# Decoder layer on one core: v goes to k's bank, y is turned a group ahead, the causal term is narrowed, the last norm's rows go to ScalarE, and the end is reordered

## The reference

```python
x = norm(x + attn(x))      # linear attention of 16 heads, then an MLP 128 -> 512 -> 128 with a gelu on a grid of 0.1
x = norm(x + xattn(x, ctx, mask))
x = norm(x + ffn(x))

# xattn: 16 heads of 8 features, 64 keys of the same batch
q, k, v = x @ WQ, ctx @ WK, ctx @ WV
scores = q @ k.T / sqrt(8)
scores = where(mask[query] or key > query, -1e9, scores)
out = (softmax(scores) @ v) @ WO

# ffn: 7 gate scores; the two largest of their softmax are divided by their sum
out = x @ W_shared.T + (w0 + w1) * (x @ W_expert.T) + bias
```

## Time and profile before

| | |
|---|---|
| median of 3 runs | 562.51 us |
| profiled execution | 561.41 us |
| its span, first to last instruction | 559.7 us |
| mean granted TensorE clock | 0.973 |
| TensorE, VectorE, ScalarE, GpSimd busy | 88%, 72%, 65%, 67% |

### The profile page before, as it was taken

How to read it: one execution, slowest core, us unless ns; L and a number is a source line. 1 busy time by engine, 2 the same in 40 slices (tenths; PEclk the granted TensorE clock), 3 DMA queues, 4 the chain that set the end, 5 groups by cost and what they waited for, 6 DMA issues and landing times. The chain is left out here.

```text
span 559.7 us, 22010 instructions
## 1 busy us (share of the span) xinstructions
PE 491.0 (88%) x8800; PEld 365.4 (65%) x8800; DVE 404.7 (72%) x1406; ACT 363.9 (65%) x685; POOL 374.7 (67%) x686
## 2 busy tenths in 40 slices
PE   2899999998999999997899999899998999998750
PEld 1777777775777767774567667676676666766530
DVE  2677777755777776556678878688887888888764
ACT  1566666555777777747777677677677676777432
POOL 6566666645577774833337878778787887879553
PEclk9999999999999999999999999899999999999775
DMA  6530000000000000002000111111201121010001
GB/s 167 169 117 2 3 2 1 4 2 1 2 0 3 1 1 1 2 7 49 17 23 4 50 51 26 28 50 50 49 6 49 51 50 50 5 51 21 22 2 57
DMA packets 24742, 17.38 MB, mean 31 GB/s; under 512 B 2112, under 2 KB 22464, under 8 KB 24640
## 3 DMA queue, kind: packets, MB, share of 16 engines
q1 hardware_dynamic: 24208, 15.90, 10.7%
q10 hardware_dynamic: 432, 0.07, 0.1%
HBM read 11.77 MB, written 4.19 MB: 29 GB/s over the span
## 5 line engine op out<-in xcount | busy, mean ns | idle before, releaser
L783 ACT ACTIVATE gel<-gel,row_scale 128x512 f32<-128x512 f32 x96 | 66.1, 720 | 29.2 <-DVE gel L1056 19.0
L790 ACT ACTIVATE gel<-pair 128x1024 f32<-128x1024 f32 x64 | 51.8, 809 | 29.0 <-PE pair L1414 28.5
L1354 PEld LDWEIGHTS pair<-w,gel 128*128 128x128 f32 x512 | 60.4, 192 | 8.0 <-issue 5.7
L1043 DVE TENSOR_REDUCE neg_max<-pair 128x16 f32<-128x1024 f32 x64 | 60.5, 945 | 5.1 <-PE pair L1368 5.0
L1354 PE MATMUL pair<-w,gel 128*128 128x128 f32 x512 | 62.4, 276 | 1.0 <-ACT gel L715 1.0
L1318 PE MATMUL pair<-hT,w 128*128 128x512 f32 x128 | 58.3, 596 | 1.3 <-ACT lev L710 1.3
L1414 PE MATMUL pair<-ident,gel 128*128 128x128 f32 x384 | 55.7, 280 | 2.9 <-ACT gel L783 1.9
L532 POOL TENSOR_SCALAR k_exp<-k_sb,quad_mask 128x512 f32<-128x512 f32 x64 | 43.0, 690 | 20.8 <-ACT k_sb L762 12.7
L1414 PEld LDWEIGHTS pair<-ident,gel 128*128 128x128 f32 x384 | 43.4, 141 | 19.1 <-issue 13.5
L1368 PE MATMUL pair<-k_exp,qT 32*32 32x128 f32 (+1 forms) x2048 | 44.5, 333 | 2.6 <-issue 2.4
L509 POOL TENSOR_TENSOR X<-X,proj_sb 128x512 f32<-128x512 f32 x16 | 20.3, 1270 | 35.6 <-ACT proj_sb L673 35.6
(11 more groups left out here) (138 smaller groups left out, 1221.9 us busy)
## 6 DMA issues: line engine op xcount, KB each, us to landing
X<-in_x SPq DMA_DIRECT2D x16, 256.0 KB, 3.1
cT<-in_ctx SPq DMA_DIRECT2D x16, 256.0 KB, 3.9
out_rows<-X SPq DMA_DIRECT2D x15, 256.0 KB, 2.4
mask_rows<-in_mask_early SPq DMA_DIRECT2D x16, 128.0 KB, 3.6
w<-in_L_attn_w SPq DMA_DIRECT2D x2, 256.0 KB, 3.4
out_rows<-X SPq DMA_DIRECT2D x2, 128.0 KB, 1.8
w_kv<-in_L_attn_wk SPq DMA_DIRECT2D x1, 64.0 KB, 3.3
w_q<-in_L_attn_wq ACTq DMA_DIRECT2D x1, 64.0 KB, 3.1
```

What stands on the lines that cost most here:

```text
L783: nc.scalar.activation(part, part, ACT.Exp, scale=row_scale[:, n:n + 1])\
L790: nc.scalar.activation(pT[par].rearrange("p (a c) -> p a c", a=2), turned, ACT.Copy)\
L1043: nc.vector.tensor_reduce(neg_max[par][:, :].rearrange("p (a h) -> p a h", a=2), scores, AX.X, ALU.max, negate=True).then_inc(max_ready, 1)
L1354: last = nc.tensor.matmul(bank(6 + q)[:, P * t:P * (t + 1)], gel[:, q, f, P * t:P * (t + 1)], w_2[:, f, :], start=(f == 0), stop=(f == NF ...
```

## The change

- v's projection writes bank 5 (k's) in 16 products of 64 columns by 64 (before: 4 of 128 by 128 to bank 4), so that both halves of the heads lie on the partitions where `v2` wants them, and `copy_v` takes 2 instructions of 64x512 in place of 4 of 64x256.
- y is turned in slot 3 for group s+2 (before: in slot 0 for group s+1), and `copy_y` on ScalarE moves with it.
- The causal term of the even tile covers the last 32 keys of each head alone. It comes last in `scores_close`; that of the odd tile comes between the two halves of `scores_open`.
- The last norm's rows (`last_rows`) are made on ScalarE for every group, in slot 1 of step s for group s-3. GpSimd makes the scale and the offset (`last_offset`). The store of a group is a step later.
- In `end`, the mixture of group 14 is done by VectorE, and `add_bias(LAST)` comes ahead of the offsets of group 14.
- `MOE_BANK` is [6, 4, 5, 5], and the waits that go with the banks are moved. In slot 0, `turn_attended` comes ahead of the `moe` product, and on ScalarE `attT` ahead of `collect`.

```diff
-MOE_BANK = [5, 6, 4, 5]
+MOE_BANK = [6, 4, 5, 5]
...
@@ phase3 and end of GpSimd
                 if exists(s - 2) and s < LAST:
                     mixture(s - 2, p)
-                    last_norm(s - 2, p)
+                    last_offset(s - 2)
...
-                mixture(LAST - 1, q)
-                end_offset(LAST - 2, rstd_c, offs_b[0])
-                end_offset(LAST - 1, rstd_b[1], offs_b[1])
+                add_bias(LAST - 1, q)
+                last_offset(LAST - 2)
                 add_bias(LAST, 2)
+                last_offset(LAST - 1)
                 pool.wait_ge(ln_c.done, LAST - 1)
-                ln_deviation(pool, ln_c, LAST, mv_c, veps_c, rstd_c)
+                ln_deviation(pool, ln_c, LAST, mv_c, veps_c, rstd_c[LAST % 2])
...
+            def last_offset(g):
+                rstd, offs = rstd_c[g % 2], offs_b[g % 2]
+                after(pool, ln_c.done, g - 1)
                 ln_deviation(pool, ln_c, g, mv_c, veps_c, rstd)
@@ copy_v and phase3 of ScalarE
-                for b in range(2):
-                    for h in range(2):
-                        batches = v2[q][h * S:(h + 1) * S, :, :, h, 0:DH] \
-                            .rearrange("p (u b) i e -> p u b i e", b=2)
-                        last = nc.scalar.activation(batches[:, :, b, :, :],
-                                                    values[b * S:(b + 1) * S, :, h, :, :], ACT.Copy)
+                for h in range(2):
+                    rows = slice(h * S, (h + 1) * S)
+                    last = nc.scalar.activation(
+                        v2[q][rows, :, :, h, 0:DH],
+                        bank(first_bank(g, 5))[rows, :].rearrange("p (b i e) -> p b i e", i=HH, e=DH),
+                        ACT.Copy)
...
-                    if t == 0 and exists(nxt):
-                        copy_y(nxt)
+                    if t == 0 and exists(s - 2):
+                        collect((s - 2) * TG + TG - 1, TG - 1, p)
...
+                    if t == TG - 1 and exists(s + 2):
+                        copy_y(s + 2)
...
+                    if t == 1 and exists(s - 3):
+                        last_rows(s - 3)
@@ end of VectorE
                 gate_weights(LAST - 1)
+                mixture(LAST - 1, q)
                 gate_top(LAST, 2)
+                last_statistics(LAST - 1, q)
                 gate_weights(LAST)
-                last_statistics(LAST - 1, q)
@@ scores on TensorE
                 for n in ns:
-                    future_scores(n)
-                for n in ns:
+                    if n % 2:
+                        future_scores(n)
                     quad_scores(n, (1, 3) if n % 2 else (0, 2)).then_inc(s_opened, 1)
...
                 for n in ns:
-                    quad_scores(n, (0, 2) if n % 2 else (1, 3)).then_inc(s_done, 1)
+                    last = quad_scores(n, (0, 2) if n % 2 else (1, 3))
+                    if n % 2:
+                        last.then_inc(s_done, 1)
+                if ns[0] % 2 == 0:
+                    future_scores(ns[0]).then_inc(s_done, 1)
...
-                for u in range(TG):
-                    last = nc.tensor.matmul(bank(first_bank(g, 4))[:, P * u:P * (u + 1)],
-                                            cT[q][:, P * u:P * (u + 1)], w_xv[:, :], start=True, stop=True)
+                for u in range(2 * TG):
+                    for h in range(2):
+                        last = nc.tensor.matmul(bank(first_bank(g, 5))[h * S:(h + 1) * S,
+                                                                       FH * u:FH * (u + 1)],
+                                                cT[q][:, S * u:S * (u + 1)],
+                                                w_xv[:, FH * h:FH * (h + 1)],
+                                                start=True, stop=True)
@@ phase3 of TensorE
-                    if t == 0 and exists(g):
-                        after(pe, moe_ready, (s - 1) * TG - 1)
-                        after(pe, v2_ready, g)
-                        turn_y(g)
...
                     if t == 2 and exists(g):
+                        pe.wait_ge(k_ready, g + 1)
+                        project_v(g, q)
+                    if t == 3 and exists(s + 2):
                         pe.wait_ge(q_ready, g + 1)
-                        project_v(g, q)
+                        turn_y(s + 2)
...
                         for u in range(TG - 1):
+                            if u == 1 and exists(g):
+                                pe.wait_ge(yT_ready, min(s + 3, NG))
```

More of the change, by code:

```diff
@@ L115, in decoder_layer @@
         veps_c = sb("veps_c", [P, TG])
-        rstd_c = sb("rstd_c", [P, TG])
+        rstd_c = [sb(f"rstd_c{i}", [P, TG]) for i in range(2)]
         negm_c = sb("negm_c", [P, TG])
@@ L411, in phase3 @@
                     load_ctx(s + 2, p)
-                if exists(s - 2) and s - 2 < LAST:
-                    store(s - 2)
-            pipeline(sp, phase3, last=NG)
+                if exists(s - 3) and s - 3 < LAST:
+                    store(s - 3)
+            pipeline(sp, phase3, last=NG + 1)
             for k, part in halves:
@@ L816, in phase3 @@
                         copy_pT(s * TG + t, t % 2)
-                    if t == 0 and exists(s - 2):
-                        collect((s - 2) * TG + TG - 1, TG - 1, p)
+                    if s == 0 and t == 0:
+                        copy_y(1)
                     if t == 0 and exists(prev):
@@ L843, in phase3, with last_rows @@
                             collect(prev * TG + u, u, q)
-            def end_rows(g, q, rstd, offs):
-                act.wait_ge(end_offs, g - LAST + 3)
+            def last_rows(g):
+                q, rstd, offs = g % 2, rstd_c[g % 2], offs_b[g % 2]
+                act.wait_ge(offs_ready, g + 1)
                 for t in range(TG):
@@ L872, in end @@
                 gate_exp(LAST)
-                end_rows(LAST - 2, p, rstd_c, offs_b[0])
-                end_rows(LAST - 1, q, rstd_b[1], offs_b[1])
+                last_rows(LAST - 2)
+                last_rows(LAST - 1)
             pipeline(act, phase1, last=NG - 2)
```

41 lines of the change are left out of this document (19 added, 22 removed).

## The result

| | median us (lowest to highest, runs) | profiled execution | its span | granted clock |
|---|---|---|---|---|
| before | 562.22 (560.33 to 564.31, 4) | 561.41 | 559.7 | 0.973 |
| changed | 570.89 (569.79 to 574.97, 4) | 571.75 | 569.7 | 0.982 |

The ratio is 1.0167, 95% interval [1.0103, 1.023]: slower by some 1.7%. 569.5 was forecast, in a range of 554 to 578.

The account below looks back on a forecast made before the run. TensorE was taken as close to the bound, with VectorE holding the first half of a step. 561.4 + 10 (15 steps) + 0.5 (last closing, first tiles) - 3.6 (end) = 568.3 us profiled; median 1.1 above, 569.5, range 554 to 578.

Parts of the forecast that it names:

- The change of shape empties the array: TensorE's opening and closing: score halves and causal term no longer overlap, 0.48 us more a pair, 0.96 a step.
- Rival A: TensorE's openings and closings: no emptying between shapes, so a step of 17.25 us and 556 us in all; chance 0.27.
- First half: Slots 0 and 1 of a step: ScalarE's copy behind four rows sets the opening, 9.4 us (8.84 before).
- VectorE's bound: First half of a step: VectorE starts at 3.09, its 6.23 us end at 9.32.
- GpSimd's part: GpSimd's mixture ends earlier and no longer holds VectorE, a gain of 0.4 us of the mean step.
- Second half: Slots 2 and 3: the turn of y in slot 3 gains little; 8.55 us (8.02 before).
- v's projection: TensorE, first half: 16 products on two column halves cost 0.15 us more, hidden; upper end 0.9 more.
- rival C: v's projection runs one after the other, 3.4 us in place of 0.9: 595 us; chance 0.06 with other large losses.
- The end: Behind the last pair: early bias removes VectorE's 3.48 us idle before the last mixture; -3.6 us.
- unexplained waits: TensorE's waits in the last phase for nothing the profile shows: 2.4 us, taken as 0.16 a step.
- My quiet step: A whole step without the unexplained waits: 9.4 + 8.55 = 17.95 us.
- Rival B: Last phase: additions cancel, VectorE alone sets the first half, a step of 17.78 us, 561 to 564 us; chance 0.10.

Follow-up runs that it names:

- e5: Kernel before with only the causal term in its new form and places: 569.56 us against before's 562.47, ratio 1.0145.
- e3: Changed kernel with the causal term in 32*32 pieces, the shape of the scores, at the same places: 579.39 us, ratio to before 1.0285.
- e4: Changed kernel with `last_rows` moved from slot 1 to the end of slot 0 on ScalarE: 567.38 us, ratio to before 1.0094.
- e2: Changed kernel with both tiles' narrow causal terms at the end of the closing, none in the opening: 566.52 us, ratio to before 1.0033.
- e12: Changed kernel with both narrow causal terms at the closing's end and `last_rows` split between slots 1 and 2: 556.77 us, ratio to before 0.9898.
- e8: Changed kernel with the turn of y and its copy back in slot 0: 575.94 us, ratio to before 1.0234.
- e9: Kernel before with only the changed order at the end of GpSimd and VectorE: 559.34 us against 562.47, ratio 0.9943.
- e1: Changed kernel with the causal term as before, both tiles' terms together ahead of the opening: 566.04 us against before's 561.52, ratio 1.0076.
- e10: Changed kernel with both narrow causal terms at the closing's end, `last_rows` in slot 0, v's projection as before: 563.49 us, ratio to before 1.0012.

## Why the prediction was right, and where it was not

**The change of shape empties the array**: right. Opening 1.19 for 1.18 forecast, closing 0.84 for 0.80, and e5 and e3 tie the cost to the term and its shape. Rival A is out: it had at most 0.8 for the opening. The pair costs 0.52 more in place of 0.48, a small miss at the closing.

**First half**: right in its mechanism, ScalarE's `copy_q`, four rows and copy in one row with VectorE close behind, but 9.13 in place of 9.4. The turn and `copy_q` come earlier than I added up: `copy_q` ended 6.64 us after the opening (449.54 - 442.90), not 6.89, and all behind it is 0.3 early. Of that, 0.1 is `weigh_values` between opening and closing: 0.67 us (444.09 to 444.76), where the trace of before has 0.78. I carried this stretch over from before as if it could not change. Another 0.1 is a second handover: both the rows and the copy start 0.1 ahead of the recorded end of the work before them, and I took off one tenth. VectorE's bound was too long in the same way, 9.32 where e5 and e4, whose first halves VectorE ends, measure 9.02 and 9.03. These lines of VectorE, before and then changed, show why:

```profile
433.93 0.29 DVE L1031 TENSOR_TENSOR att<-pair,rec 128x128 f32<-128x128 f32 x1
445.70 1.23 DVE L1044 TENSOR_REDUCE neg_max<-pair 128x16 f32<-128x1024 f32 x1 [0.16 <-PE pair L1385]
```

Before, the reduction at 434.36 followed VectorE's own work with no idle time, so part of the 0.92 behind the start of the closing was that work. I added the closing's 0.21 to it, for 1.13; it is 0.94 (445.70 - 444.76).

**GpSimd's part**: true and small. The waits fell from 12.7 to 4.5 us. But this is no reserve: when e2 and e12 shortened the step, the waits for GpSimd came back (9.7 us in 9 waits, 13.5 in 11).

**Second half**: 8.54, forecast 8.55. The turn of y costs what it wins, as its removal from slot 3 (e8: 8.43) bears out to 0.11.

**v's projection**: 0.09 more, hidden, as forecast; rival C is out.

**The end**: right, and helped by luck in the profiled execution. The forecast was -3.6, and +0.5 for the last closing and the first tiles; measured alone it is -3.5 in the span of e9 and -3.1 in its median. The profiled span of the changed kernel has -4.8 with the last closing in it, 1.7 more than forecast, and 1.4 of that goes with the granted clock behind the last opening, as the ends of the other kernels show.

**The term that was too small**: the sum took TensorE's issue waits as a constant 0.16 a step, "with the 2.4 / 15 = 0.16 of unexplained waits". Even before they were 3.4, and they went to 8.9 us; with the rest that lies beyond quiet steps the changed kernel has 11.7 us where the sum had 2.4, 9.3 too little. My quiet step was too long by 17.95 - 17.67 = 0.28, 4.2 us in 15 steps, and the end was too long by 1.7. The three leave 3.4, and that is what the profiled execution missed by: 571.75 against 568.3. In the median only 1.4 is left, 569.5 against 570.9, because I added 1.1 to get from the profiled execution to the median, and now the profiled one lies 0.9 above it. So the hit is closer than the parts deserve: the mechanism at the openings was right, and two errors of size and the choice of execution cancel. With the stops at 0.16 a step, as I had them, and the measured quiet step, the step would be 17.83 and the median some 565 by my other terms.

By medians the causal term is +7.1 (e5, alone in before) or 4.9 (e1, undone in the changed kernel), and the end is -3.1 (e9). With e5's value, 4.7 of the +8.7 are left for the rest of the change. No experiment separates them into work, stops and clock. Why the stops' sum differs between kernels with the same instructions on TensorE (8.9 and 4.8 us, the changed kernel and e4) stays open.

**Rival B** (additions cancel, 561 to 564) was nearer in the undisturbed step than my forecast: 17.67 and 0.16 make 17.83, where it had 17.78 and I had 18.1. The rows do fit better than I thought, though ScalarE and not VectorE ends the first half, and the second is 8.54 in place of 8.3. Its time fell on the stops.

## What to carry to other kernels

Count the changes of tile shape on TensorE, not the columns: here a term of half the width, placed between pieces of another shape, cost 0.5 us a pair more than the wide one ahead of all, and the same narrow terms put together at the end cost no more than the wide one (e2: 1.46 us a pair against 1.50). Where two engines end a half step within 0.15 us of each other, as here, an edit that frees one wins little (0.10 us in e4) until the other is freed as well, and a piece of work can be moved too early (e10) as well as too late. Read the issue waits of the busiest engine for the kernel before, all of them, and give them a term with a wide range: they were 4.8 to 11.2 us in kernels here with 9184 matmul instructions each. And compare the granted clock stretch by stretch before a difference between two profiled executions is put down to an edit.

## What was not expected of the hardware

- TensorE stops of 0.2 to 2.9 us for nothing that the profile shows. One long one stands at the same instruction in two kernels with the same stream, and is gone from there when 128 instructions are put ahead. Their sum is 3.4 to 14.5 us in programs of 8800 to 9568 matmul instructions.
- Granted clock of 0.50 in stretches of 3.4 or 6.8 us, 3.4 to 20.5 us of the last phase in all. Six products that take 1.64 us at the full clock took 2.37 in one.
- Pieces of the same shape on other rows of the array start within 0.07 to 0.11 us of each other, float32 beside bf16; a change from 32\*128 to 32\*32 costs 0.10 to 0.11.
- 32 instructions of 128x64 on two column halves (16 products) take 1.15 us (1.06 for 8 of 128x128), with the same work in all: the halves run side by side though each uses all rows. The Trainium skill (TensorE: Matmul & The Clock Gate, Part 3) has weight loads overlap running products only when the row group differs. Here they share it, and the 32 weight loads take 1.01 us of the same 1.15; the measurement decides against the rule.
- The same 64 instructions of `weigh_values` take 0.67 us behind the split opening and 0.77 to 0.78 behind one that ends in 32 pieces of scores. No experiment looked into it.
